# A six-block decoder in one kernel: encoder steps in another order, top-k masks, keys and first scores made earlier, row statistics summed by ScalarE

## What is computed

```python
# block 4, for each of 4 layers: at each of 112 positions the 16 sequences attend to each other
qkv = einsum('bsd,ed->bse', xb, Wqkv[l]) + bqkv[l]
attn = softmax(scores + mask);  o = attn @ v;  o = o @ Wo.T + bo
xb = layernorm(xb + o, g1, be1)
ff = relu(xb @ W1.T + b1) @ W2.T + b2
xb = layernorm(xb + ff, g2, be2)
# block 5, its beginning
Q = x_text @ Wq;  K = x_vision @ Wk                       # 4 heads of 32
scores = Q K^T / sqrt(32);  topv, topi = top_k(scores, 32)
attn = scatter(softmax(topv));  c_t = mean_heads(attn) @ (x_vision @ Wv)
x = layernorm(x_text)                                     # rows of 256 features
x = x * (1 + gate * scale_in) + gate * shift_in           # from c_t
```

## Time and profile before

| | us |
|---|---|
| median of 3 runs | 2418.9 (2416.46 to 2422.77) |
| the profiled execution | 2417.03 |
| its span | 2415.2 |
| busy PE / DVE / POOL / ACT | 2096.2 / 1532.5 / 811.6 / 701.6 |
| chain that ended last | PE 66%, DVE 21%, POOL 5%, ACT 3%, issue 3%, DMA 2% |
| encoder, first to last step | about 886 to 1748 |
| top-k part on VectorE | from 1765 |

### The profile page before, as it was taken

How to read it: one execution, slowest core, us unless ns; L and a number is a source line. 1 busy time by engine, 2 the same in 40 slices (tenths; PEclk the granted TensorE clock), 3 DMA queues, 4 the chain that set the end, 5 groups by cost and what they waited for, 6 DMA issues and landing times.

```text
span 2415.2 us, 37733 instructions
## 1 busy us (share of the span) xinstructions
PE 2096.2 (87%) x15300; PEld 1468.4 (61%) x15300; DVE 1532.5 (63%) x3079; ACT 701.6 (29%) x1351; POOL 811.6 (34%) x729
## 2 busy tenths in 40 slices
PE   6988989999999978999999999987667677879986
PEld 2333347777666657888788878776535455446632
DVE  7998945556343325555555555566389989737556
ACT  6445324343212222222222222222122222121232
POOL 3243339966400025444444444433081000013201
PEclk7768789999899989999999999999866757989998
DMA  5212172222010037001000100100061101220001
GB/s 153 77 67 96 61 164 83 59 72 60 5 53 1 1 116 171 11 1 68 1 1 26 44 1 1 51 1 1 1 159 29 35 25 33 67 68 1 0 1 31
DMA packets 67182, 114.48 MB, mean 47 GB/s; under 512 B 34153, under 2 KB 58722, under 8 KB 65794
## 3 DMA queue, kind: packets, MB, share of 16 engines
q1 hardware_dynamic: 67010, 112.07, 16.2%
HBM read 91.56 MB, written 33.34 MB: 52 GB/s over the span
## 4 chain that ended last, share of the span: by engine, by line
PE 66%; DVE 21%; POOL 5%; ACT 3%; issue 3%; DMA 2%; SPq 1%; POOLq 0%; DVEq 0%; ACTq 0%
PE PS L1529 8%; PE PS L1545 8%; PE PS L1278 5%; PE PS L1256 4%; DVE top L2286 4%; PE PS L1446 4%; DVE w_s L2295 4%; PE PS L2173 2%; PE PS L2163 2%; PE PS L2102 2%; PE PS L1474 2%; PE PS L1504 2%; PE PS L1556 2%; DVE st_h L689 2%; PE PS L877 2%
## 5 line engine op out<-in xcount | busy, mean ns | idle before, releaser
L287 POOL TENSOR_SCALAR ln_ve<-ln_mv 128x2 f32<-128x2 f32 (+1 forms) x91 | 21.8, 240 | 1157.0 <-DVE ln_mv L271 1156.9
L1728 DVE TENSOR_TENSOR p_x<-PS,cols 128x1024 f32<-128x1024 f32 x112 | 129.3, 1216 | 147.9 <-PE PS L1491 147.8
L1792 POOL TENSOR_TENSOR q_x<-q_f,cols 128x2048 f32<-128x2048 f32 x56 | 208.7, 3745 | 11.2 <-ACT q_f L1646 11.2
L1087 DVE TENSOR_REDUCE XD<-PS 112x2 f32<-112x750 f32 x128 | 119.8, 939 | 95.7 <-PE PS L877 95.2
L455 PE MATMUL PS<-bc_parts,ident 96*128 96x448 bf16 x256 | 105.4, 516 | 43.1 <-DVE st_h L689 28.9
L1046 ACT ACTIVATE e_t<-PS 125x672 f32<-125x672 f32 x128 | 93.6, 731 | 158.0 <-PE PS L890 158.0
L1335 DVE SCALAR_TENSOR_TENSOR XA<-PS,gate_w,XA 112x256 f32<-112x256 f32 x128 | 56.0, 479 | 125.6 <-PE PS L1278 125.6
L877 PE MATMUL PS<-enc_w,q_s 32*112 32x375 f32 x512 | 131.1, 538 | 2.2 <-DVE XD L1087 2.2
L1616 ACT ACTIVATE wb<-PS,cols 128x256 f32<-128x256 f32 x224 | 91.0, 473 | 139.7 <-PE PS L1529 139.7
L2062 PE MATMUL PS<-dg,e_p 112*125 112x112 f32 x384 | 78.3, 394 | 60.4 <-ACT dg L2241 60.4
L890 PE MATMUL PS<-q_s,enc_w 32*125 32x112 f32 x1536 | 123.3, 291 | 2.6 <-ACT e_t L1046 2.6
(11 more groups left out here) (357 smaller groups left out, 4715.2 us busy)
## 6 DMA issues: line engine op xcount, KB each, us to landing
k_full_scratch<-k_scratch SPq DMA_DIRECT2D x112, 112.0 KB, 2.9
v_all_scratch<-v_st SPq DMA_DIRECT2D x16, 750.0 KB
v_t<-v_all_scratch SPq DMA_DIRECT2D x16, 750.0 KB
t_ring<-k_full_scratch SPq DMA_DIRECT2D x8, 784.0 KB, 15.4
enc_w<-in_enc_w SPq DMA_DIRECT2D x2, 3072.0 KB, 11.3
wc<-in_enc_w SPq DMA_DIRECT2D x2, 3072.0 KB, 11.4
k_all_scratch<-k_st SPq DMA_DIRECT2D x16, 375.0 KB
enc_w<-k_all_scratch SPq DMA_DIRECT2D x64, 93.8 KB, 3.5
```

The lines of the kernel that those rows point to most:

```text
L1087: dve.tensor_reduce(nm_w[0:T, g % 4, 64 * half + 16:64 * half + 49:32], PS[0:T, 2 * half:2 * half + 2, 0:S2], AX.X, ALU.max, negate=True). ...
L1728: last = dve.tensor_tensor(p_x[:, m, :, :, :], ps[1][:, m * P:(m + 1) * P].rearrange("p (h i) -> p h i", i=16).unsqueeze(2) .to_broadcast( ...
L1792: last = pool.tensor_tensor(q_x[:, c, :, :].rearrange("p t (h i) -> p t h i", i=16), q_f[:, k % 2, c, :].rearrange("p (t i) -> p t i", i=1 ...
```

## The change

- Encoder, TensorE: `qkv` is split into `queries_or_keys(i, 0)`, `queries_or_keys(i, 1)` and `values_of(i)`. Queries of step k+1 are made between `weigh(k-1)` and `project(k-1)`; keys stay; values come behind the turn of x1.
- Encoder, ScalarE: the query copy comes first in the loop, and the copy of the turned x1 ahead of the softmax exponential.
- In the loop's turn k = 28 VectorE does `first_norm(27)` ahead of `second_norm(26)`, GpSimd's roots follow, and in turn 29 TensorE turns the second norm of step 26 behind x1 of step 27.
- Top-k: masks are loaded and prepared during the last encoder steps, the keys of batch 0 are made ahead of the last turn. After `XF` is complete come two query groups, the scores of batch 0, the other two groups, the keys of batch 1, and only then the turn of the rows. SyncE loads the context of batches 0 and 1 after the last projection, and issues `e_w1` when `XF` is complete.
- Row statistics: VectorE's 16 are gone. ScalarE copies each row block once with a running sum and squares it once with a running sum (32 instructions, between heads 1 and 2 of batch 0); GpSimd makes mean and root of all 16 from these sums.

```diff
-            def qkv(i):
+            def queries_or_keys(i, j):
...
+            def values_of(i):
...
+            queries_or_keys(0, 0)
             for k in range(STEPS + 3):
+                if k == STEPS + 2:
+                    pe.wait_ge(e_loaded, 32)
+                    topk_keys(pe, 0)
                 if 0 <= k - 1 < STEPS:
                     scores(k - 1)
-                if 0 <= k - 3 < STEPS:
...
+                if 0 <= k - 3 < STEPS and k != STEPS + 1:
+                    turn_second(k - 3)
                 if 0 <= k - 1 < STEPS:
                     turn_scores(k - 1)
                 if k < STEPS:
-                    qkv(k)
-                if k == 0:
-                    turn_residuals()
+                    queries_or_keys(k, 1)
                 if 0 <= k - 2 < STEPS:
                     pe.wait_ge(n1_done, k - 1)
                     pe.wait_ge(eu_copied, k - 1)
                     turn(2, x1[:, k % 2, :, :]).then_inc(ex_ready, 1)
+                if k < STEPS:
+                    values_of(k)
+                if k == 0:
+                    turn_residuals()
+                if k == STEPS + 1:
+                    turn_second(k - 3)
...
                 if 0 <= k - 1 < STEPS:
                     weigh(k - 1)
+                if k + 1 < STEPS:
+                    queries_or_keys(k + 1, 0)
+                if 0 <= k - 1 < STEPS:
                     project(k - 1)
 
-            pe.wait_ge(ez_copied, STEPS)
-            for j in range(B // 2):
...
-                if 0 <= k - 2 < STEPS:
...
+                if 0 <= k - 2 < STEPS and k != STEPS:
+                    second_norm(k - 2)
                 if 0 <= k - 1 < STEPS:
...
+                    first_norm(k - 1)
+                if k == STEPS:
+                    second_norm(k - 2)
...
-            sp.wait_ge(xa_copied, B // 2)
+            sp.wait_ge(ew_ready, STEPS)
             sp.wait_ge(e_prep, 1)
...
                 if b == 1:
+                    sp.wait_ge(ez_copied, STEPS)
                     sp.dma_start(wc[:, 0:5250], dr["e_w1"]).then_inc(ew1_loaded, 16)
...
+            queries(0)
+            queries(1)
             pe.wait_ge(e_prep, 3)
-            keys(0)
             scores(0)
+            queries(2)
+            queries(3)
+            topk_keys(pe, 1)
+            for j in range(B // 2):
+                turn_rows(j)
...
+            def copy_rows(j):
+                bank = m_bank(act, "x", j)
+                for m in range(2):
+                    b, half = 2 * j + m, bank[0:T, m * D:(m + 1) * D]
+                    act.activation(XA[0:T, b, :], half, ACT.Copy, accum_out=row_sum[:, b:b + 1])
+                    last = act.activation(half, half, ACT.Square, accum_out=row_sq[:, b:b + 1])
+                last.then_inc(m_used, 1)
+
             for b in range(B):
                 for h in range(XH):
                     n = XH * b + h
+                    if n == 2:
+                        copy_keys(1)
+                        for j in range(B // 2):
+                            copy_rows(j)
...
-            for q in range(NQ):
-                dve.wait_ge(xa_copied, 2 * (q + 1))
-                norm_stats(dve, link, [XA[0:T, q * QB + i, :] for i in range(QB)])
```

More of the change, by code:

```diff
@@ L1624, in enc_act @@
             for k in range(STEPS + 3):
+                if k < STEPS:
+                    layer = k // ROUNDS
+                    act.wait_ge(eq_ready, 2 * k + 1)
+                    for c in range(KC):
+                        last = act.activation(q_f[:, k % 2, c, :], ps[4][:, c * RT:(c + 1) * RT], ACT.Identity,
+                                              bias=bq4[:, 2 * layer + c:2 * layer + c + 1], scale=0.25)
+                    last.then_inc(eq_copied, 1)
                 if 0 <= k - 1 < STEPS:
@@ L1642, in enc_act @@
                 if k < STEPS:
-                    layer = k // ROUNDS
-                    act.wait_ge(eq_ready, 2 * k + 1)
-                    for c in range(KC):
-                        last = act.activation(q_f[:, k % 2, c, :], ps[4][:, c * RT:(c + 1) * RT], ACT.Identity,
-                                              bias=bq4[:, 2 * layer + c:2 * layer + c + 1], scale=0.25)
-                    last.then_inc(eq_copied, 1)
                     act.wait_ge(eq_ready, 2 * k + 2)
@@ L1693, in normed, with second_norm, first_norm @@
                 return last
+            def second_norm(i):
+                layer, r = divmod(i, ROUNDS)
+                x = xg[:, 2 * r:2 * r + 2, :]
+                dve.wait_ge(x1_biased, i + 1)
+                dve.wait_ge(eg_ready, i + 1)
+                dve.tensor_tensor(x, ps[3].rearrange("p (g d) -> p g d", d=D), x1[:, i % 2, :, :], ALU.add)\
+                    .then_inc(eg_added, 1)
+                dve.wait_ge(eg_added, i + 1)
+                link(normed(x))
+                if layer < LAYERS - 1:
+                    affine(layer, x, "g2", "be2", n2_done)
+                else:
+                    affine(layer, x, "g2", "be2", None)
+                    link(dve.tensor_tensor(x, x, xg0[:, 2 * r:2 * r + 2, :], ALU.add))
+                    normed(x).then_inc(n2_done, 1)
+            def first_norm(i):
+                layer, r = divmod(i, ROUNDS)
+                x = x1[:, i % 2, :, :]
+                dve.wait_ge(xg_biased, i + 1)
+                dve.wait_ge(ew_ready, i + 1)
+                dve.tensor_tensor(x, ps[6].rearrange("p (g d) -> p g d", d=D), xg[:, 2 * r:2 * r + 2, :],
+                                  ALU.add).then_inc(ew_added, 1)
+                dve.wait_ge(ew_added, i + 1)
+                link(normed(x))
+                affine(layer, x, "g1", "be1", n1_done)
             for k in range(STEPS + 2):
@@ L2024, in m_bank, with topk_keys, topk_masks, queries @@
             return ps[4 + n % 4]
+        def topk_keys(pe, b):
+            bank = m_claim(pe, "k", b)
+            pe.wait_ge(ctx_loaded[b % 2], 32 * (B // 2 + b // 2 + 1))
+            for i in range(2):
+                last = pe.matmul(bank[:, 0:S2], e_wk[0:CR[i], i, :], ctx_f[0:CR[i], b % 2, i, :],
+                                 start=(i == 0), stop=(i == 1))
+            last.then_inc(m_ready, 1)
+        def topk_masks(pool):
+            pool.wait_ge(ew_ready, STEPS)
+            pool.memset(msk8[:, :], 1).then_inc(e_prep, 1)
+            pool.wait_ge(em_loaded, 16 * (XH + 1))
+            pool.wait_ge(e_prep, 1)
+            pool.tensor_scalar(mskb[:, :], msk8[:, :], -1.0, -FAR, ALU.add, ALU.mult).then_inc(e_prep, 1)
+            pool.tensor_scalar(tmk[:, :], tmk8[:, :], 1.0, None, ALU.mult).then_inc(e_prep, 1)
         def s4x_pe(pe):
-            pe.wait_ge(e_loaded, 32)
-            pe.wait_ge(xa_copied, B // 2)
-            for q in range(NQ):
+            pe.wait_ge(ez_copied, STEPS)
+            def queries(q):
                 bank = m_claim(pe, "q", q)
@@ L2034, in s4x_pe, with turn_rows @@
                 last.then_inc(m_ready, 1)
-            def keys(b):
-                bank = m_claim(pe, "k", b)
-                pe.wait_ge(ctx_loaded[b % 2], 32 * (B // 2 + b // 2 + 1))
-                for i in range(2):
-                    last = pe.matmul(bank[:, 0:S2], e_wk[0:CR[i], i, :], ctx_f[0:CR[i], b % 2, i, :],
-                                     start=(i == 0), stop=(i == 1))
+            def turn_rows(j):
+                bank = m_claim(pe, "x", j)
+                for m in range(2):
+                    for c in range(KC):
+                        last = pe.transpose(bank[0:T, m * D + c * P:m * D + (c + 1) * P],
+                                            XF[:, c, (2 * j + m) * T:(2 * j + m + 1) * T], ident[:, :])
                 last.then_inc(m_ready, 1)
             def scores(b):
-                pe.wait_ge(m_used, m_count("k", b) + 1)
+                pe.wait_ge(m_used, max(m_count("k", b), m_count("q", b // QB)) + 1)
                 for h in range(XH):
```

125 lines of the change are left out of this document (47 added, 78 removed).

## The result

| | before | after |
|---|---|---|
| median, us | 2417.71 (4 runs, 2416.46 to 2422.77) | 2396.61 (4 runs, 2395.67 to 2398.17) |
| span of the profiled execution | 2415.2 | 2394.2 |

What follows compares the result with a forecast made beforehand. TensorE bounds the encoder's regular part, VectorE the top-k. Terms 23.1 + 1.0 + 0.5 - 5.6 + 5.6 = 24.6 us off 2417.03, plus 1.9 to the runs' median, give 2394; range 2382 to 2406.

Steps and rivals of the forecast that it cites:

- Regular steps: Encoder's first three layers: step falls from 28.64 to 27.6-27.7 us; 22 x 1.05 = 23.1 us gained, bounds 20.7-24.2.
- The cover for the softmax scaling: Regular encoder step: VectorE's softmax scaling, up to 4.19 long, still ends before the probabilities' turn; cover 1.4 us wide.
- The one ahead of them: The encoder step ahead of the 21 regular ones: counted as a 22nd step gaining the same 1.05 us.
- Last layer: Encoder's last layer: four steps gain 0.25 each, 1.0 us; the step without new queries gains 0.5 us.
- Last step: Last encoder step: feed product waits for second_norm(26), starting about 28.3 after the previous one; 5.6 us lost, bounds 5-8.
- Start of the top-k: Top-k start: first scores 11 us earlier, less 5 stall and 1.5 collisions, plus 1.1 removed wait: 5.6 us gained.
- The stall for the sums: Top-k start: VectorE waits for exponentials queued behind ScalarE's 32 row-sum instructions; 4 to 10 us, taken as 5.
- Collisions and the removed wait: Top-k start: GpSimd's normalisation beside VectorE's masked sums costs 1.5 us; exponentials no longer behind late keys gain 1.1.
- rival A: Top-k start: ScalarE's sums cheap (0.31 to 0.4 each), no VectorE stall, 10 to 13 gained; 2388 us, chance 0.22.
- B: Regular steps: longer norm chain leaves half of each step's gain as a wait before x1's turn; 2405 us, chance 0.13.
- C: Last feed product wholly at the lower clock and ScalarE's sums at 0.7 or more each; 2405 us, chance 0.08.
- D: Regular steps: TensorE's clock falls in each step, 35 us on top; 2429 us, slower than before, chance 0.03.

Runs made afterwards that it cites:

- e1: The kernel after with second_norm(26) again ahead of first_norm(27) in the last encoder step, on all engines; 2389.5 us, ratio 0.9856 to before.
- e2: The kernel after with the turn of second(26) and its two copies moved behind the last feed product; 2386.3 us, ratio 0.9844 to before.
- e10: The kernel after with GpSimd's row products in pieces of 256 columns in place of 1024; 2393.8 us, ratio 0.9878 to before.
- e14: The kernel after with plain row copies on ScalarE and row statistics on VectorE ahead of batches 1 to 4; 2400.0 us, ratio 0.9896 to before.
- e5: The kernel after with the x1 turn behind values again and ScalarE's x1 copy behind the exponential again; 2409.5 us, ratio 0.9946 to before.
- e7: The kernel after without GpSimd's ten row products and sums (g_in, b_in) on the normalised rows; 2390.7 us, ratio 0.9867 to before.

## Why the prediction came out as it did

**Regular steps: right, term a little small.** The starts came as worked out: `project` at F + 10.72 (10.70 forecast), `first_norm` at 12.72 (12.8), the turn of x1 at 17.86 (17.9), the clock at 1.00. The step is 27.43, not 27.6 to 27.7, because the first feed product, which no longer waits for its copy, takes 7.07 and not 7.17, and the turn of x1 takes 0.50 of the path and not 0.6. 21 steps gained 25.6, above my bound of 24.2. The cover for the softmax scaling was not needed there (0.71).

**"The one ahead of them": wrong.** I counted 22 steps. The start does not gain: from the first product to the first F it took 50.7 to 51.7 (mean 51.2) in the three profiles with the old encoder order and 52.3 to 53.3 (mean 52.8) in the ten with the new. The 22nd step is -0.8 in this pair and -1.6 on the mean instead of 1.05: before, the queries of step 1 ran behind the first scores, now they stand ahead of them, and those scores start 14.3 after the first product instead of 12.8.

**Last layer: 1.5 forecast, 3.6 measured.** 0.34 a step (30.91 to 30.57) where I had 0.25, and 0.6 in the step without new queries, as worked out (0.5). The rest is 1.6 that I had not claimed: the first long step, 32.51 with the granted clock at 0.95 in the earlier trace rows, is 30.57 after. That is luck and not the change: in other profiles of the new order (e1, e2, e10, e14) a step of 32.2 stands later instead, and in e5 the first is 32.6.

**Last step: right, 6.8 for 5.6.** The feed product came at F + 29.5 (28.3 forecast) for the reason given, and took 8.70. The step that I had short is the norm application of 2.01: GpSimd's b2 addition, which waits for the turn of x1 and now comes right behind the norm's root, fell onto it, 1.3 longer, which is the missing 1.2. In the profiles of the new order this step is 37.8 to 39.3, so neither the 5.6 nor the 6.8 is exact to 1. I took the swap as such for the loss; e2 shows that it is a gain of 4 to 6 with the turn elsewhere.

**Start of the top-k: right, then lost by a term I had not seen.** First scores came 10.8 earlier (11). The stall for the sums was 0.88, not 5: a sum takes 0.37 and not 0.42 to 0.6, and the batch left more room than 23 - 12.5. Collisions and the removed wait together cost 1.8 net (0.4 forecast). Had that been all, 8.1 would have stayed, rival A in part. My estimate from the figures of the Trainium skill (ScalarE: Activation LUTs, What ACT_TABLE_LOAD costs) was 306 ns a sum and a stall of 0 to 1. The stall of 0.88 agrees; the 306 ns do not, since a sum takes 0.37 here, with a read of the accumulator (0.19) as an instruction of its own.

The step that failed is that I stopped at batch 2 and took every later batch as unchanged. The rows for it were there: before has one wait of 5.21 (in batch 8), and a wait that stands in one of three like places depends on something that the change can move. It cost 6.2.

**The sum.** Against the forecast the start and the regular steps brought 1.4 more, the last layer 2.1 more, the last step 1.2 less, the top-k 3.8 less (1.8 for 5.6) and the rest 1.9 less. That 24.6 forecast and 21 measured lie so close is in part luck: the misses point both ways, and without the second event the gain would have been 27, about as far off on the other side.

**Rivals.** A's premise (cheap sums) was right, and its 6 were eaten by the event. B: the wait ahead of the turn is 0.28, so it fell. C: feed and top-k both lost more, by 1.2 and 3.8, for other reasons than named (the last feed product took 8.70 against 8.60 before). D: the clock stayed at 1.00 in all regular steps.

**Rest.** 1.9 more after the top-k is within what unchanged code varies between profiles here (343.6 to 346.3), so I give it no cause. The queries' first start lies between 883.9 and 891.7 in the profiles, ahead of anything changed; that is scatter that each time carries.

## What to carry to other kernels

Fill a wait with independent work only up to the point where nothing queued behind it gets later: a moved step (here the turn of second(26)) costs by what stands behind it on its engine, not by its own length. When the granted clock has two levels, look at each periodic product at the low level, and ask whether the queue behind it still meets its time; a wait in one of several like places is a warning. A long two-input instruction of GpSimd beside a VectorE path is best cut in pieces: it gave 6.2 us here, and that GpSimd then needs about 2.9 instead of 2.35 for the same columns cost nothing, since it is off the path.

## What the runs showed of the hardware

**VectorE waits for a whole GpSimd instruction, but not for each kind.** Masked sums (two SBUF inputs) were held by GpSimd's TENSOR_TENSOR until its end plus 0.4, in all six cases of after. No sum was held so by GpSimd's TENSOR_SCALAR on 256 columns: twelve sums of after, e7 and e10 started while one was under way, and eleven took 0.54 to 0.55, one 0.64. In e7 a TENSOR_SCALAR at 1767.66 took 1.22, the sum at 1768.47 took 0.54, and the next GpSimd instruction took 1.62 instead of 1.22. Spans on GpSimd are rough in the profile. The Trainium skill (SBUF — State Buffer, SBUF: two separate sides) calls the port pair an exclusive lock for the whole instruction, taken by whichever starts first; for GpSimd's two-input instruction the trace agrees, for the one-input instruction it does not.

**A norm application with one SBUF tensor was held as well**: L282, 2.01 for two instead of 0.73, beside GpSimd's two-input addition of 1.26. The Trainium skill (SBUF — State Buffer, Who interferes with whom) says that a tensor_scalar of VectorE can run in a mode that takes the shared pair; the trace agrees in so far as this one was held, and no row shows in which mode it ran.

**ScalarE's running sum costs a second instruction**: ACTIVATE 0.38 and the read of the accumulator 0.19 for 256 columns, 0.37 from one to the next.

**TensorE's low level.** In the top-k TensorE's granted clock moved between 0.50 and 1.00 (0.66 on the mean) while the engine idled for VectorE in each batch; one `values(q)` took 7.20 at 0.50 and 3.83 at 1.00, and in its old place VectorE waited 5.2 behind every one at the low level (18) and behind none at the high one (12).
